# Last MLP stage of a two-layer vision tower on one core: two of six rounding steps on GpSimd, the last stores on two queues

## What is computed

```python
a1, a2 = alpha_a1.mean(), alpha_a2.mean()
xq = round(clip(layernorm(h) / a1, -8, 7))
x1 = (xq @ wq1.T) * alpha_w1 * a1 + b1            # 768 hidden values per token
x1 = clip(gelu(x1), -10, 10)
hq = round(clip(x1 / a2, -8, 7))                  # the rounding that the change moves in part
out = h + (hq @ wq2.T) * alpha_w2 * a2 + b2       # 192 values per token
```

## Time and profile before

| | |
|---|---|
| median of 3 runs | 2405.19 us |
| profiled execution, its own time | 2403.57 us |
| its span, first to last instruction | 2401.8 us |
| busy share of the span: PE, DVE, ACT, POOL | 90%, 82%, 85%, 70% |
| mean granted clock of PE | 0.988 of full speed |
| last stage in the span | about 2182 to 2402 us |
| adds of POOL in the last stage (L1656) | 50 instructions, 57 to 58 us |
| output stores (L1668) | 160 DMAs |

### The profile page before, as it was taken

One profiled execution on the slowest core, in us unless ns is written; L12 is line 12 of the kernel. 1 busy time (PEld: TensorE's weight loads), 2 busy tenths in 40 slices (PEclk: granted clock), 3 DMA queues, 4 the chain that ended last, 5 costly groups with the idle time before them and its releaser, 6 DMA issues. The chain is left out here.

```text
span 2401.8 us, 76354 instructions
## 1 busy us (share of the span) xinstructions
PE 2168.1 (90%) x25422; PEld 1700.2 (71%) x25422; DVE 1979.7 (82%) x4966; ACT 2034.0 (85%) x5745; POOL 1672.2 (70%) x2165
## 2 busy tenths in 40 slices
PE   5899999999999799999999999999999999988876
PEld 5788885888878577777777777777777777765554
DVE  5666776888787689899989989999899999976875
ACT  4677776777776599999999999999999999996997
POOL 5667761333332488989899999989899999992323
PEclk9899999999999999999999999999999999999999
DMA  6334420000100276666666666666666666671111
GB/s 189 92 110 120 120 71 28 6 5 5 44 15 5 35 122 125 119 123 121 120 121 121 122 119 126 119 121 120 124 120 124 121 121 119 122 119 40 53 51 54
DMA packets 734155, 222.64 MB, mean 93 GB/s; under 512 B 667590, under 2 KB 732720, under 8 KB 733808
## 3 DMA queue, kind: packets, MB, share of 16 engines
q1 hardware_dynamic: 734064, 221.56, 45.0%
HBM read 46.49 MB, written 9.68 MB: 23 GB/s over the span
## 5 line engine op out<-in xcount | busy, mean ns | idle before, releaser
L1516 POOL TENSOR_TENSOR b_pr<-b_pr,fc 128x394 f32<-128x394 f32 (+1 forms) x768 | 651.5, 868 | 122.2 <-DVE fc L1436 122.2
L1365 ACT ACTIVATE b_pr<-b_scores,fc 128x197 f32<-128x197 f32 (+1 forms) x1536 | 630.2, 437 | 2.4 <-issue 1.2
L1501 POOL TENSOR_TENSOR b_halves<-b_pr,b_halves 128x394 f16<-128x394 f32 (+1 forms) x640 | 564.8, 908 | 31.0 <-ACT b_halves L1334 27.0
L1273 PE MATMUL b_banks<-fp,wqkv 128*128 128x197 f16 x3840 | 377.5, 249 | 42.7 <-DVE b_qk L1420 38.6
L1430 DVE TENSOR_REDUCE fc<-b_scores 128x2 f32<-128x394 f32 x768 | 395.9, 557 | 4.0 <-PE b_scores L1291 1.9
L1273 PEld LDWEIGHTS b_banks<-fp,wqkv 128*128 128x128 f16 x3840 | 319.7, 98 | 83.9 <-DVE b_qk L1420 60.5
L1334 ACT ACTIVATE b_halves<-b_pr 128x788 f16<-128x788 f32 x384 | 341.3, 889 | 4.7 <-POOL b_pr L1516 4.7
L1365 ACT ACTIVATION_READ_ACCUMULATOR b_pr<-b_scores,fc 128x1 f32 (+1 forms) x1536 | 337.5, 220 | 0.0
L977 POOL TENSOR_TENSOR h<-h,fp_bias 69x192 f32 (+3 forms) x128 | 133.4, 1070 | 266.8 <-DVE m_xn L139 266.8
L1420 DVE SCALAR_TENSOR_TENSOR b_qk<-b_banks,b_qk 128x394 f16<-128x394 f32 x384 | 215.0, 560 | 99.9 <-ACT b_qk L1348 99.7
L1280 PE MATMUL b_banks<-wqkv,fp 128*128 128x384 f16 (+1 forms) x1280 | 254.6, 330 | 40.4 <-DVE h L1455 38.8
(11 more groups left out here) (251 smaller groups left out, 4387.2 us busy)
## 6 DMA issues: line engine op xcount, KB each, us to landing
patches<-in_x SPq DMA_DIRECT2D x64, 588.0 KB, 4.3
b_pt<-b_halves SPq DMA_TRANSPOSE x384, 3.2
out<-z_res SPq DMA_DIRECT2D x64, 96.0 KB
fc<-b_halves SPq DMA_TRANSPOSE x192, 3.2
fp<-b_halves SPq DMA_TRANSPOSE x192, 3.2
m_raw_weights<-in_wqkv SPq DMA_DIRECT2D x2, 1152.0 KB, 6.9
out<-z_res SPq DMA_DIRECT2D x32, 51.8 KB
h<-h SPq DMA_DIRECT2D x32, 44.2 KB
```

What stands on the lines that cost most here:

```text
L1273: last = t.matmul(out[:, g * SEQ:(g + 1) * SEQ], w[:, (2 * n + g) * P:(2 * n + g + 1) * P], x, start=(j == 0), stop=(j == 4))
L1365: last = nc.scalar.activation(pr[n % 3][0:ROWS[c], c, e, :], scores[n % 2][0:ROWS[c], e, c * SEQ:(c + 1) * SEQ], ACT.Exp, bias=nmx[n % 2][ ...
L1501: nc.gpsimd.tensor_tensor(halves[n % 3][0:ROWS[c], c, 1, :, 0:SEQ], pr[n % 3][0:ROWS[c], c], halves[n % 3][0:ROWS[c], c, 0, :, 0:SEQ], ALU ...
L1516: last = nc.gpsimd.tensor_tensor(p, p, inv, ALU.mult)
```

## The change

In each group the rounding of chunks 1 and 4 moves from ACT to POOL, as a `tensor_scalar` (multiply, add) with the same numbers. The semaphore of the roundings is split in two, one for each engine, and gelu, which needs the rounding of chunk c - 4, asks `rounded` which to wait for. On POOL, the rounding of chunk 1 stands ahead of the residual add, that of chunk 4 behind it. PE's down waits for both semaphores. Of the last group's stores, those of tiles 1 and 3 are issued by ACT, the others by SP as before.

```diff
+        ON_POOL = (1, 4)
+        ON_SCALAR = [f for f in range(HC) if f not in ON_POOL]
+        def rounded(c):
+            g, f = divmod(c, HC)
+            signal, by = (done_by_p, ON_POOL) if f in ON_POOL else (done_by_s, ON_SCALAR)
+            return signal, len(by) * g + by.index(f) + 1
...
-                in_turn([(add_stream, 0)])
+                def round_chunk(f):
+                    def make(g):
+                        n = starts(g)[-1]
+                        pool.wait_ge(clipped, HC * g + f + 1)
+                        if f == ON_POOL[0] and g >= 2:
+                            pool.wait_ge(made_y, g - 1)
+                        nc.gpsimd.tensor_scalar(hid[g % 2][:, f, 0:n], act_out[(HC * g + f) % 4][:, 0:n], S["inv_a2"][:, 0:1],
+                                                ROUND + float(LOW_BITS), ALU.mult, ALU.add).then_inc(done_by_p, 1)
+                    return make
+                in_turn([(round_chunk(ON_POOL[0]), 1), (add_stream, -1), (round_chunk(ON_POOL[1]), 1)])
...
                 def store(g):
...
+                            if g == count - 1 and k % 2:
+                                continue
...
                 def round_chunk(g, f):
+                    if f in ON_POOL:
+                        return
...
-                            act.wait_ge(hid_done, c - 3)
+                            act.wait_ge(*rounded(c - 4))
...
+                last = count - 1
+                act.wait_ge(h_done, count)
+                for k in (1, 3):
+                    for i, lo, hi, row in pieces(groups[last][k]):
+                        act.dma_start(out[i, lo:hi, :], res[last % 2][row:row + hi - lo, k, :]).then_inc(stored[last % 2], 16)
...
-                    pe.wait_ge(hid_done, HC * g + HC)
+                    pe.wait_ge(done_by_s, len(ON_SCALAR) * (g + 1))
+                    pe.wait_ge(done_by_p, len(ON_POOL) * (g + 1))
```

More of the change, by code:

```diff
@@ L1579, in mlp_1 @@
         stored = [sem(f"z_stored{b}") for b in range(2)]
-        (xn_made, quantised, turned, xt_done, fc_made, gelu_made, clipped, hid_done, made_y, scaled, h_done, scaled_rstd) = map(sem, (
-            "z_xn_made", "z_quantised", "z_turned", "z_xt_done", "z_fc_made", "z_gelu_made", "z_clipped", "z_hid_done",
+        (xn_made, quantised, turned, xt_done, fc_made, gelu_made, clipped, done_by_s, done_by_p, made_y, scaled, h_done, scaled_rstd) = map(sem, (
+            "z_xn_made", "z_quantised", "z_turned", "z_xt_done", "z_fc_made", "z_gelu_made", "z_clipped", "z_done_by_s", "z_done_by_p",
             "z_made_y", "z_scaled", "z_h_done", "z_scaled_rstd"))
@@ L1683, in round_chunk @@
                     nc.scalar.activation(hid[g % 2][:, f, 0:n], act_out[(HC * g + f) % 4][:, 0:n], ACT.Copy, scale=S["inv_a2"][:, 0:1],
-                                         bias=ROUND + float(LOW_BITS)).then_inc(hid_done, 1)
+                                         bias=ROUND + float(LOW_BITS)).then_inc(done_by_s, 1)
                 def gelu(g):
```

## The result

The changed kernel takes 2391.32 us, the median of 5 runs (2390.77 to 2393.82), against 2405.19 (5 runs, 2402.74 to 2406.37). The ratio is 0.9944, with a 95% interval from 0.993 to 0.9957: 13.9 us faster by the medians, where 9.1 were forecast. The profiled execution has a span of 2389.0 us, 12.8 less than before.

The account below looks back on a forecast made before the run. ACT was taken to bound the kernel; after the change DVE, held up by POOL, sets a 7.29 us step. Terms 4.9 + 1.2 + 0.6 + 1.0 + 1.4 = 9.1 us, so 2405.19 - 9.1 = 2396 us, range 2389 to 2408.

Parts of the forecast that it names:

- What bounds the kernel: Last stage, steady groups: ACT's gelus and roundings, without a pause, set the group step of 7.67 us.
- DVE's sum: DVE's slots per group: 6.18 us, plus 0.69 at clip 4 and a wait at quantise, giving a 7.29 us step.
- d - 0.28: Time a DVE instruction loses behind a POOL instruction of length d; a POOL rounding was taken as d = 0.70 us.
- the chain forecast at 13.83: Gelu, clip, finish, PE's up and next gelu through two groups, even with engines free: 13.83 us, 6.92 each.
- The rival without hindrance: DVE and POOL hinder each other no more than now: step 6.92 us, gain 15.6, time 2390; chance 0.13.
- To the last add: Stage end, 9.67 us up to the last residual add: PE, finish and adds in turn, gain 0.
- The four steps to the left-over group: Steps from 2271.38 to 2301.18, 29.80 us, smaller group among them: gain 0.3 each, 1.2 us.
- The start: Stage start to 2209.85: three roundings fewer ahead of gelu 5 of the second group, gain 1.4 us.
- the eight steps: Steady group steps in the stage's first half, 61.53 us before: forecast gain 3.0 us, at 0.38 a steady step.
- the block of 0.42: At the stage start, one block of 0.42 us subtracted from the 1.83 us gained by three fewer roundings.
- The two steps behind the stores: Two steps to 2335.26, 16.49 us, where the pipeline refills after the 32 stores: gain 0.3 each, 0.6 us.
- The stores: Stage end: ACT issuing two of five stores gains 0, as one DMA engine works till the end; other end 1.2.

## Why the prediction was right, and where its sizes were off

**What bounds the kernel.** Right. ACT's sum set the step at 7.67, and DVE's sum with POOL's instructions in it sets it now: every one of DVE's instructions follows the last one in the steady rows.

**DVE's sum.** Right in each term: 0.69 at clip 4 (1.23 for 0.54), 0.38 at quantise (forecast d - 0.28 = 0.42), nothing in finish, d = 0.69 for 0.70. That makes 7.24 where 7.29 was forecast. The doubled roundings showed the terms one by one, and the kernel nearly without adds showed what stands behind them: 13.62 us for two groups, near the chain forecast at 13.83. One reason was empty: POOL's adds had not been seen to stretch finish because in the kernel before none ever ran beneath it. The row that bore on it was the step to `xt`, which reads PSUM too and takes 0.68 us with an add beneath it. After the change finish takes 1.01 us with a rounding beneath it, as it did without. The sum rested on the lock that the Trainium skill's "SBUF — State Buffer", section "Who interferes with whom", describes, and 0.35 to 0.38 per rounding in the way, 0.00 beneath finish, fits it; but a DVE instruction held up loses some 0.3 us less than the length of POOL's. The rival without hindrance (2390) came nearest to the measured 2391.3, but for a wrong reason: its step of 6.92 isn't there. That the measured time is nearer to it than to the forecast 2396 comes from the terms below and from scatter.

**Where the sum was short by 3 us in the stage.** Three terms were mis-sized.
- *To the last add: 0 forecast, 0.90 measured.* The windows of the two kernels, columns as above, show one part. Before:

```profile
2380.00:2382.00 2.00, 1.00 (x7) 0.83 (x7) 1.47 (x4) 2.00 (x5) 0.91 (x1) 0.81 0.03 10
2382.00:2384.00 2.00, 2.00 (x15) 1.88 (x14) 1.09 (x2) 2.00 (x5) 1.49 (x2) 0.50 0.00 0
```

After:

```profile
2370.00:2372.00 2.00, 2.00 (x25) 1.79 (x22) 1.57 (x2) 2.00 (x5) 1.62 (x3) 1.00 0.01 2
```

  PE's clock stood at 0.50, the 1.2 GHz level, in the down of the last group but one before (15 matmuls in 2 us), and at full speed in the same place after (25 in 2 us). I had read that stretch as PE, finish and adds in turn and had not read its clock. The kernel with the stores alone has the old roundings and ran this step at full clock in 5.11 us, where the kernel before took 5.66 and the changed one takes 4.77. So about 0.55 of the 0.90 are the clock's and 0.34 the change's: finish stands behind the last clips too, and these wait for ACT's gelus and roundings, which I had left out. Whether the change brings the clock's part in each run isn't shown.
- *The four steps to the left-over group: 1.2 forecast, 2.19 measured.* Three of them gained 0.64, 0.15 and 0.44, together 1.23. The fourth gained 0.96, and it is the one that stood at a clock of 0.79 before (8.00 us) and at 1.00 after (7.04). In it ACT had waited 0.64 us for PE before. How much of the 0.96 the change alone would have given isn't shown, since no run has the old roundings at full clock there.
- *The start: 1.4 for 1.82, and the eight steps 3.0 for 3.6.* Three roundings are 1.83 us, so the block of 0.42 that I took off doesn't show at the start; why isn't shown. The second is the 0.05 us a step by which d - 0.28 and the slots were too high, and a first step of 7.24 where it had been 7.85.

The two steps behind the stores gained less than forecast (0.17 for 0.6). The changed kernel's profile had more time at half clock there; with the roundings alone the same two steps took 15.26 us, 1.23 less than before. So in this pair of profiles the clock gave 0.55 us and up to 0.96 in two places and took about 1.4 in a third, and that the stage's gain of 12.2 holds so little of it is luck. 0.64 us came from stages that the change doesn't touch, and the rest of the 13.9 by the medians is of the size of their scatter.

**The stores.** Right: 11.04 and 11.07 us, alone 0.9994. The 1.2 us that I kept as the other end wasn't there either.

## What to carry to other kernels

Before moving work from a full engine to an idle one, sum up the other engines' slots in the stage, start to start, and price each POOL instruction by what runs on DVE at that moment: beneath an instruction that reads PSUM (finish, the step to `xt`) it was free, and in front of a clip or a normalising step from SBUF it cost its length less 0.3 us. That an engine is only 26% busy is no measure of the room it has. Where a stage ends on stores, look at how many DMA engines are at work in the last microseconds before giving the issue to a second queue: row counts in multiples of 16 took 4.2 us off the end, counted from the last add but one, and the second queue nothing. And before you explain why one step is longer than the same step of another kernel, read PE's clock in both.

## What the runs showed of the hardware beyond this

A `tensor_scalar` with two operations on 128 x 512 float32 takes 0.69 us on POOL, 0.53 with 320 columns; from these two an estimate is 0.83 ns an element and 0.26 us of fixed cost. Where POOL and DVE both had instructions ready, they took turns: of two roundings in a row, each held up another instruction of quantise (four take 1.99 us, with one rounding 1.61, with none 1.24). One core's earlier stages, unchanged, put the start of the last stage anywhere between 2180.06 and 2185.51 us, while the stage repeats within a tenth of a microsecond in its steady part. So differences under 5 us are better read from the stage than from the time, and those of 1 to 2 us only from stretches in which PE's clock is the same: down of one group took 2.80 us of PE at full clock and 4.29 and 4.45 where its mean clock was about 0.7.
